# A gated two-layer block: inverse roots on GpSimd, scatters without pacing, and 8-bit rounding in the feed-forward

## The chip, the cores and the metric

The kernel runs on one core of a Trainium2 chip. The metric is the device time of one launch in microseconds (us). The kernel before takes 2155.1 us, the median of 3 runs (2150.84 to 2159.89).

Engines go by their short names: PE is TensorE (PEld its weight loads), DVE is VectorE, ACT is ScalarE, POOL is GpSimd, SP is SyncE. Each runs its own stream of instructions in program order and waits on semaphores that other engines raise.

## The reference

64 blocks of 128 tokens with 256 features, and as much context, go through two layers, each an attention over the context and a feed-forward:

```python
x = x + tanh(g_xattn[0]) * L0_xattn(layernorm(x), ctx, ctx)       # 16 heads of 16, softmax over 128 keys
x = x + tanh(g_ffn[0])   * L0_ffn(layernorm(x))                   # 64 experts, top 8, capacity 256, shared expert
x = x + tanh(g_xattn[1]) * L1_xattn(layernorm(x), ctx, ctx, mask) # the same with a mask
x = x + tanh(g_ffn[1])   * L1_ffn(layernorm(x))                   # 8-bit fake quantisation, 704 inner features

def _layernorm(x): return (x - mean(x)) / sqrt(var(x) + 1e-5)
def _act_fake_quant(x, clip_factor):
    scale = sigmoid(clip_factor) * max(abs(x)) / 127.0
    return clip(round(x / scale), -128.0, 127.0) * scale
xq = _act_fake_quant(x, clip_x)
h = _act_fake_quant(silu(xq @ wq(w_gate).T) * (xq @ wq(w_up).T), clip_down)
out = h @ wq(w_down).T
```

## The kernel before

The program has five stages, one after the other.

- **Start and layer 1's attention (to about 980 us).** 64 blocks pass through a software pipeline. In each *slot* every engine does a different piece of work for a different block: a stage `m` has its scores, the stages from `k` to `u` each hold an older one. A slot, read from one `mt` reduce of DVE (L793, the row maximum of the scores) to the next, holds on PE: scores (L346), V projection (L445), head sums (L476), shared expert's down projection (L536), transposes (L410), a second copy of the scores, transposed (L363), transposes of the head output (L486), of the maxima (L379) and of the normalised rows (L496), Q and K projections (L430), output projection (L463/L465), shared expert's up projections (L513), router logits (L525), probabilities by values (L393), counts of tokens by expert (L547/L548). ACT copies PSUM to SBUF between them (`xn` L637, `vx` L627, `pay` L651, `xt` L602, `at` L669, `x2t` L678), takes the exponential (L594) and the router's `en` (L688). DVE has maxima, residuals, statistics and the router's top 8.
- **Scatters.** For each block POOL issues 8 indirect DMAs (L1922), one for each of a token's experts, that write 128 rows of 1 KB each into the experts' buffers. Before each of the 8 stands a wait on a different semaphore of PE (the list `steps`), so that the 8 are spread over the slot. Before the first scatter POOL clears the buffers (L1905, 16 DMAs of 1032 KB, in pairs of which each waits for the last) and then two accumulators (L1909).
- **The inverse root of the variance.** `inverses` (L861 on) works on 2 columns, one for the block that enters and one for a block that leaves attention. It adds epsilon (`var`, L870) and then takes 11 small DVE instructions: a bit trick for a first value and three Newton steps, each waiting for the last; the last gives `rstd` (L890). `nmr` (L894) follows, and ACT's `xn` and `pay` wait for it. The planner of the DVE stream is the hand-written `body`: `norming(n)` puts n of these steps at a place, `routing(n)` n of the router's steps, `dispatching()` one of the three that turn counts into row numbers.
- **Experts (about 980 to 1270 us)**, with a scatter-add of results (L1407).
- **Layer 2's attention (about 1280 to 1930 us)** is the same pipeline without router, shared expert and scatters, and with a mask added on PE (L330). POOL has one small addition for each block (L1936).
- **Feed-forward, pass 0 (about 1935 to 2055 us)**, 16 chunks of 512 tokens: ACT scales by the quantiser's factor and adds 12582912.0, by which fp32 rounds; POOL clips and subtracts the constant again (two instructions over 128x2048, the second writes bf16); PE computes gate and up; DVE has three products and three maxima of the hidden values for each chunk.
- **Feed-forward, pass 1 (about 2057 to 2149 us)**, per chunk: ACT scales and rounds six slices of the hidden values (L1649); for four of them DVE adds the lower bound and subtracts the constant (`floored`, L1699, two instructions), then caps (L1708); for the other two POOL clips (L1674) and ACT subtracts (L1657); PE does 24 matmuls (L1736); DVE scales the result (L1716, four instructions), POOL adds the residual (L1680, four).

The wait that paces the scatters, and the order of DVE's stream around the root:

```python
steps = (("qk_done_0", ahead(b, 7)), ("o_done_0", ahead(b, 4)), ...
for n in range(TOPK):
    pool.wait_ge(sem(steps[n][0]), steps[n][1])
    G.indirect_dma_start(...)
...
variances(n, y); norming(5); routing(1); norming(2); routing(1); norming(2); routing(1); norming(1)
silu(w); norming(2); silu_up(w); norming(1)
```

## Time and profile before

| | us |
|---|---|
| median of 3 runs | 2155.1 |
| profiled execution, its own time | 2150.62 |
| its span in the profile | 2148.9 |
| mean granted TensorE clock | 0.954 of full |
| PE busy | 1825.1 (85%) |
| DVE busy | 1583.3 (74%) |
| ACT busy | 1117.6 (52%) |
| POOL busy | 900.0 (42%) |

"Span" is the time from the first to the last instruction that the profile has; the execution's own time is 1.7 us longer. Busy time is an average over stages with different limits, so the stages have to be read apart. In rows of the time line the bracket says how long the engine was idle before the instruction, and what it waited for; `remote` is a releaser that the profile does not name, `issue` an engine that waited for nothing that the profile shows.

### The profile page before, as it was taken

Reading aid. Unit: us, or ns where it says so; the run is one execution under the profiler, and the core shown is the slowest. Engines: PE = TensorE matmul, PEld = TensorE weight load, DVE = VectorE, ACT = ScalarE, POOL = GpSimd, SP = SyncE. Lnnn points to the kernel's source line nnn. Section 1 sums busy time; section 2 is a strip of 40 time slices with the busy share of each in tenths; the row PEclk is TensorE's granted clock in tenths of the full one; section 3 lists DMA queues with packets and bytes.
Section 4 is the critical chain, followed back from the end, with each engine's and each line's share of the span. In section 5 each row is a group of like instructions: output and inputs, shape, how many; then the busy total and the mean of one; then the engine's idle time right before and its main releaser. Section 6 shows DMA issues by size and latency. Waiting matters only on the chain.

```text
span 2148.9 us, 56605 instructions
## 1 busy us (share of the span) xinstructions
PE 1825.1 (85%) x20848; PEld 1451.8 (68%) x20848; DVE 1583.3 (74%) x6070; ACT 1117.6 (52%) x2299; POOL 900.0 (42%) x844
## 2 busy tenths in 40 slices
PE   5998888888889889746999978999999999968856
PEld 3777777777777777636888856676676667643334
DVE  5788888888888888772444447787887878778977
ACT  2555555555555555412222225666666666648877
POOL 1255555555555555574777750000000000005558
PEclk8999999999999999967999989999999999999988
DMA  9821111121111111045999951111111111102355
GB/s 234 217 80 56 53 51 48 48 68 53 41 36 43 43 42 38 22 138 127 225 210 219 208 102 40 46 39 45 40 41 43 39 46 39 31 24 108 127 204 188
DMA packets 184178, 187.98 MB, mean 87 GB/s; under 512 B 37042, under 2 KB 166613, under 8 KB 181856
## 3 DMA queue, kind: packets, MB, share of 16 engines
q1 hardware_dynamic: 136384, 142.69, 21.5%
q0 software_dynamic: 47520, 41.67, 10.5%
q8 instruction: 168, 2.75, 0.5%
q14 instruction: 106, 0.87, 0.1%
HBM read 103.72 MB, written 140.77 MB: 114 GB/s over the span
## 4 chain that ended last, share of the span: by engine, by line
PE 35%; DVE 30%; another core or an unknown queue 10%; issue 9%; DMA 7%; ACT 4%; POOL 4%; SPq 1%; POOLq 0%; ACTq 0%; DVEq 0%
DVE mt L793 8%; DMA accumulator<-ye,tid 6%; PE bank L513 5%; PE tiles L363 4%; PE bank L393 4%; PE tiles L346 3%; PE bank L476 3%; PE bank L465 2%; PE bank L445 2%; DVE hmax L1617 2%; POOL accumulator L1407 2%; PE bank L536 2%; DVE qm L805 2%; DVE newton L880 2%
## 5 line engine op out<-in xcount | busy, mean ns | idle before, releaser
L1922 POOL DMA_INDIRECT expert_rows<-pay,idx x512 | 503.7, 984 | 374.8 <-issue 107.8
L793 DVE TENSOR_REDUCE mt<-tiles 128x16 f32<-128x2048 f32 x128 | 293.5, 2293 | 49.6 <-PE tiles L346 37.1
L1936 POOL TENSOR_TENSOR res<-res,bias 128x256 f32<-128x256 f32 x64 | 46.3, 724 | 573.4 <-ACT xn L637 573.4
L594 ACT ACTIVATE pt<-tiles 128x2048 f32<-128x2048 f32 x128 | 241.6, 1887 | 44.3 <-PE tiles L363 44.1
L1407 POOL DMA_INDIRECT accumulator<-ye,tid x128 | 198.5, 1551 | 93.7 <-DMA accumulator<-ye,tid 34.8
L617 ACT ACTIVATE qkp<-bank,kb,keep 128x128 f32<-128x128 f32 x500 | 205.1, 475 | 0.0
L363 PE MATMUL tiles<-qm,qkp 32*128 32x128 f32 x4096 | 152.6, 286 | 40.1 <-DVE mt L793 36.9
L363 PEld LDWEIGHTS tiles<-qm,qkp 32*128 32x128 f32 x4096 | 127.8, 188 | 69.3 <-DVE mt L793 50.3
L430 PE MATMUL bank<-xt,w_q 128*128 128x128 f32 x1024 | 167.1, 287 | 3.2 <-issue 2.2
L393 PE MATMUL bank<-pt,vx 128*32 128x128 f32 x4096 | 160.2, 277 | 11.1 <-issue 9.1
L430 PE MATMUL bank<-cxax,w_k 128*128 128x128 f32 x1000 | 156.8, 279 | 0.6 <-issue 0.6
L669 ACT COPY at<-bank 128x256 f32<-128x256 f32 x128 | 47.7, 372 | 210.5 <-remote 183.7
L805 DVE SCALAR_TENSOR_TENSOR qm<-bank,keep,qkp 128x256 f32<-128x256 f32 x256 | 112.1, 479 | 59.0 <-remote 54.6
L430 PEld LDWEIGHTS bank<-xt,w_q 128*128 128x128 f32 x1024 | 138.6, 196 | 25.0 <-issue 23.1
L346 PE MATMUL tiles<-qkp 32*128 32x256 f32 x2048 | 150.1, 407 | 2.9 <-ACT qkp L617 2.9
L445 PE MATMUL bank<-w_v,cxax 128*128 128x256 f32 x500 | 137.5, 398 | 3.1 <-DMA res<-in_x 3.1
L1372 DVE TENSOR_SCALAR ye<-bank,wcol 128x256 f32<-128x256 f32 x128 | 56.0, 479 | 113.1 <-PE bank L1263 112.5
L393 PEld LDWEIGHTS bank<-pt,vx 128*32 128x32 f32 x4096 | 114.7, 110 | 34.8 <-issue 15.7
L430 PEld LDWEIGHTS bank<-cxax,w_k 128*128 128x128 f32 x1000 | 135.1, 195 | 1.8 <-issue 1.5
L465 PE MATMUL bank<-w_o,at 128*128 128x256 f32 x512 | 134.6, 386 | 0.5 <-ACT at L669 0.5
L660 ACT COPY ovs<-bank 128x512 f32<-128x512 f32 x128 | 75.1, 587 | 92.5 <-PE bank L393 92.5
L346 PEld LDWEIGHTS tiles<-qkp 32*128 32x128 f32 x2048 | 93.6, 187 | 27.7 <-issue 17.7
(263 smaller groups left out, 4175.0 us busy)
## 6 DMA issues: line engine op xcount, KB each, us to landing
expert_rows<-zt POOLq DMA_DIRECT2D x16, 1032.0 KB
xr<-expert_rows SPq DMA_DIRECT2D x64, 258.0 KB
cxax<-in_ctx SPq DMA_DIRECT2D x128, 128.0 KB
cxax<-accumulator SPq DMA_DIRECT2D x128, 128.0 KB, 2.2
hidden_away<-h_ring SPq DMA_DIRECT2D x8, 1536.0 KB, 5.0
res<-in_x SPq DMA_DIRECT2D x64, 128.0 KB
accumulator<-xa SPq DMA_DIRECT2D x64, 128.0 KB
accumulator<-zt SPq DMA_DIRECT2D x64, 128.0 KB
```

The lines of the kernel that those rows point to most:

```text
L346: last = nc.tensor.matmul(both, qt[r % 2][rows, j, :], kp[r][rows, :, j, :], start=(L == 0), stop=True, skip_group_check=(L == 1))
L363: last = nc.tensor.matmul(tiles[:, i, n * P:(n + 1) * P], kp[r][rows, e, j, :], qm[rows, e, j, :], start=(L == 0), stop=True, skip_group_c ...
L393: last = nc.tensor.matmul(bank[7][32 * h:32 * h + 32, g * P:(g + 1) * P], vx[r][:, GH * g + h, :], pt[p][:, i, n * P:(n + 1) * P], start=T ...
L430: last = nc.tensor.matmul(o_, w[:, c, j * P:(j + 1) * P], (cx[r] if n else xt[p])[:, c, :], start=(c == 0), stop=(c == KC - 1))
L445: last = nc.tensor.matmul(bk[:, 0:D], cx[r][:, c, :], w_v[:, c, :], start=(c == 0), stop=(c == KC - 1))
L465: last = nc.tensor.matmul(bank[6][:, 0:D], at[r % 2][:, c, :], w_o[:, c, :], start=(L == 1 and c == 0), stop=(c == KC - 1))
L594: nc.scalar.activation(pt[r % 2][:, :, :], tiles[:, :, :], ACT.Exp).then_inc(sem(sm("exp_done")), 1)
L617: last = nc.scalar.activation(kp[r][:, e, j, :], bank[5][:, (KC + j) * P:(KC + j + 1) * P], ACT.Identity, bias=kb[:, e, j:j + 1], scale=ke ...
L793: nc.vector.tensor_reduce(mt[:, :].rearrange("p (i n c) -> p i n c", i=RT, n=2 * KC)[:, :, :, 0], tiles[:, :, :].rearrange("p i (n k) -> p ...
L805: last = nc.vector.scalar_tensor_tensor(qm[:, e, :, :], bank[4 if L == 0 else 6][:, 0:P].unsqueeze(1).broadcast_to([P, KC, P]), keep[:, 1 ...
L1407: nc.gpsimd.indirect_dma_start(out=acc[p][:, :], out_offset=bass.IndirectOffsetOnAxis(ap=tid[r][:, h:h + 1], axis=0), in_=ye[r][:, h, :], ...
L1922: G.indirect_dma_start(out=xe[:, :], out_offset=bass.IndirectOffsetOnAxis(ap=idx[r][:, n:n + 1], axis=0), in_=pay[r][:, :], in_offset=None ...
```

## The change

Four parts.

1. **Inverse roots.** The 11 Newton instructions on DVE go, in both layers. DVE computes `var`; POOL takes `var` to the power -0.5 (one `tensor_tensor` with `ALU.pow` on 128x2, L1844) and DVE waits for it ahead of `nmr`. In the first layer POOL's stream has the power of the entering block ahead of the scatters of the block six slots older; in the second it stands ahead of L1936's addition.
2. **Scatters.** The waits on PE in front of them go; the only one left is for the block's row numbers. The clears of the experts' buffers are spread over the first slots between the powers, two pairs ahead.
3. **Order in layer 1.** PE's counts (now L549/L550) move behind the scores, into bank 5 and one slot later; V's projection (L447) moves behind the head sums (L478), into bank 4, and now waits for `silu_done` and `qm_done`; the transposes wait for `v_out` in their place. DVE takes the `mt` maximum ahead of the dispatch steps, and the router's steps stand earlier (8 of them in a row before the residual).
4. **Feed-forward.** ACT writes rounded values directly as 8-bit integers, which rounds and clips; the addition of 12582912.0, POOL's clips, and ACT's L1657 go. POOL turns pass 0's integers into bf16 with one copy instead of two instructions; in pass 1 DVE has three copies (of two slices each, 128x1024) in place of L1699's two and L1708's one. In pass 1 the stages also lie one chunk closer together.

```diff
             def transposes(f):
...
                 if L == 0:
-                    wait(pe, sm("silu_done"), b - 4)
-                    wait(pe, sm("qm_done"), b - 1)
+                    pe.wait_ge(sem(sm("v_out")), b + 1)
...
             def body(stage):
...
                 if L == 0:
+                    moe_counts(u)
+                    heads_to_tokens(o)
                     project_v(f)
-                    heads_to_tokens(o)
                     moe_down(v)
...
                     values(k)
-                    moe_counts(v)
@@ inverses
                 st.mark(V.tensor_scalar(var[:, :], mv[:, :, 1], EPS, None, ALU.add))
                 yield
-                st.need()
-                st.mark(V.tensor_scalar(root[:, :].bitcast(i32), var[:, :].bitcast(i32), 1, None, ALU.arith_shift_right))
...
+                dve.wait_ge(sem(sm("rstd_step")), NORM_STEPS * s1 + 2)
+                st.k += 1
                 st.mark(V.scalar_tensor_tensor(nmr[:, :], mv[:, :, 0], -1.0, rstd[:, :], ALU.mult, ALU.mult))
@@ DVE body, layer 1, then layer 2
-                    routing(3)
+                    routing(1)
...
-                    routing(5)
+                    routing(8)
...
                     variances(n, y)
-                    norming(5)
-                    routing(1)
...
                     norming(1)
+                    routing(1)
                     silu(w)
-                    norming(2)
                     silu_up(w)
                     norming(1)
...
                     variances(n, y)
-                    norming(11)
+                    norming(1)
                     shifted(m)
-                    norming(2)
+                    norming(1)
@@ POOL
+            def inverse_roots(eng, L, s):
+                if s >= NB + PAIR[L]:
+                    return
+                eng.wait_ge(sem(f"rstd_step_{L}"), NORM_STEPS * s + 1)
+                wait(eng, f"xn1_done_{L}", min(s, NB))
+                wait(eng, f"xn2_done_{L}", s - PAIR[L])
+                G.tensor_tensor(rstd[:, :], var[:, :], minus_half[:, :], ALU.pow).then_inc(sem(f"rstd_step_{L}"), 1)
...
                 for n in range(TOPK):
-                    pool.wait_ge(sem(steps[n][0]), steps[n][1])
                     G.indirect_dma_start(out=xe[:, :], ...
...
-            attention_slots(lambda stage: scatter(stage(6)))
+            for s in range(FIRST[0], NB + LAGS):
+                inverse_roots(pool, 0, s - FIRST[0])
+                zero_rows(s - FIRST[0] + ZEROED_AHEAD)
+                if s >= LAGS:
+                    scatter((s - LAGS, (s - LAGS) % 4))
@@ feed-forward
-                nc.scalar.activation(slot_of(k)[:, i, :], slot_of(k)[:, i, :], ACT.Copy, bias=RND, scale=s_guq[:, i:i + 1]
+                if i % 2 == 0:
+                    wait(act, "f_whole", IC // 2 * (k - 2) + i // 2 + 1)
+                nc.scalar.activation(h_i[k % 2][:, i, :], slot_of(k)[:, i, :], ACT.Copy, scale=s_guq[:, i:i + 1]
...
-                nc.gpsimd.tensor_scalar(h, h, RND + QMAX, RND - QMAX - 1.0, ALU.min, ALU.max).then_inc(sem("f_clipped"), 1)
...
+                V.tensor_copy(f_q[k % 2][:, 2 * p:2 * p + 2, :], h_i[k % 2][:, 2 * p:2 * p + 2, :]).then_inc(sem("f_whole"), 1)
```

POOL's stream in the middle of layer 1, before: one block's eight scatters.

```order
L1922 DMA expert_rows<-pay,idx 16384x258 [waits qk_done_0,slot_step_0]
L1922 DMA expert_rows<-pay,idx 16384x258 [waits o_done_0]
L1922 DMA expert_rows<-pay,idx 16384x258 [waits up_done_0]
L1922 DMA expert_rows<-pay,idx 16384x258 [waits pv_done_0]
L1922 DMA expert_rows<-pay,idx 16384x258 [waits s_done_0]
L1922 DMA expert_rows<-pay,idx 16384x258 [waits down_done_0]
L1922 DMA expert_rows<-pay,idx 16384x258 [waits v_done_0]
L1922 DMA expert_rows<-pay,idx 16384x258 [waits st_done_0]
```

POOL's stream there in the changed kernel, two blocks.

```order
L1844 TENSOR_TENSOR rstd<-var,minus_half 128x2 [waits xn2_done_0,xn1_done_0,rstd_step_0]
L1868 DMA expert_rows<-pay,idx 16384x258 [waits slot_step_0]
L1868 DMA expert_rows<-pay,idx 16384x258 x7
L1844 TENSOR_TENSOR rstd<-var,minus_half 128x2 [waits xn2_done_0,xn1_done_0,rstd_step_0]
L1868 DMA expert_rows<-pay,idx 16384x258 [waits slot_step_0]
L1868 DMA expert_rows<-pay,idx 16384x258 x7
```

Eight scatters now stand in a row behind each power, with no wait on PE between them.

PE's stream at the start of a slot of layer 1, before, from the values (L393) to the transposes.

```order
L393 MATMUL bank<-pt,vx 32x128 x15
L547 MATMUL bank<-sel,strict_tri 128x64 [waits en_out_0,sel_done_0]
L548 MATMUL bank<-sel,ones_e 128x64
L346 MATMUL tiles<-qkp 128x2x128 [waits qk_out_0,exp_done_0]
L346 MATMUL tiles<-qkp 128x2x128 x3
L346 MATMUL tiles<-qkp 128x2x128 [waits qk_out_0]
L346 MATMUL tiles<-qkp 128x2x128 x3
L445 MATMUL bank<-w_v,cxax 128x256 [waits qk_out_0,tile_in0]
L445 MATMUL bank<-w_v,cxax 128x256
L476 MATMUL bank<-ident,ovs 128x128 [waits ov_out_0]
L476 MATMUL bank<-ident,ovs 128x128 x3
L536 MATMUL bank<-w_sd,ht 128x256 [waits pos_done_0,silu_done_0]
```

The same stretch in the changed kernel.

```order
L397 MATMUL bank<-pt,vx 32x128 x15
L350 MATMUL tiles<-qkp 128x2x128 [waits qk_out_0,exp_done_0]
L350 MATMUL tiles<-qkp 128x2x128 x3
L350 MATMUL tiles<-qkp 128x2x128 [waits qk_out_0]
L350 MATMUL tiles<-qkp 128x2x128 x3
L549 MATMUL bank<-sel,strict_tri 128x64 [waits qk_out_0,sel_done_0]
L550 MATMUL bank<-sel,ones_e 128x64
L478 MATMUL bank<-ident,ovs 128x128 [waits ov_out_0]
L478 MATMUL bank<-ident,ovs 128x128 x3
L447 MATMUL bank<-w_v,cxax 128x256 [waits qm_done_0,silu_done_0,tile_in0]
L447 MATMUL bank<-w_v,cxax 128x256
L538 MATMUL bank<-w_sd,ht 128x256 [waits en_out_0,silu_done_0]
```

The counts no longer stand between the values and the scores, and V's projection is behind the head sums.

## Rows read from the trace of the kernel before

**Rows 1.** Windows: slots of layer 1 (56 together in one), of layer 2, two chunks.
```profile
core 0: us, PE busy (x) PEld busy (x) DVE busy (x) ACT busy (x) POOL busy (x), PEclk, DMA share, GB/s
85.07:96.64 11.57, 11.57 (x143) 10.19 (x144) 10.92 (x58) 7.31 (x17) 2.44 (x4) 1.00 0.75 197
96.64:115.01 18.37, 15.23 (x143) 12.80 (x144) 11.80 (x59) 6.97 (x16) 10.72 (x11) 0.81 0.37 127
502.23:515.96 13.73, 12.20 (x144) 10.41 (x143) 11.43 (x58) 7.19 (x16) 7.80 (x9) 1.00 0.17 46
115.01:890.37 775.36, 689.49 (x7953) 587.24 (x7954) 638.05 (x3191) 405.09 (x898) 435.93 (x449) 1.00 0.17 48
1499.59:1509.45 9.86, 9.20 (x147) 6.89 (x146) 7.88 (x27) 6.30 (x13) 0.73 (x1) 1.00 0.15 42
2124.55:2134.88 10.33, 7.05 (x48) 5.33 (x48) 8.29 (x16) 9.47 (x14) 9.79 (x10) 0.83 0.31 103
```

**Rows 2.** Time line, POOL, first train of scatters; start, duration, idle before.
```profile
96.52 1.08 POOL L1922 DMA_INDIRECT expert_rows<-pay,idx  x1 [0.30 <-issue]
...
104.33 0.97 POOL L1922 DMA_INDIRECT expert_rows<-pay,idx  x1 [0.31 <-issue]
...
505.18 0.97 POOL L1922 DMA_INDIRECT expert_rows<-pay,idx  x1 [1.24 <-PE bank L536]
```

**Rows 3.** Time line, ACT, around the same scatters.
```profile
89.09 0.37 ACT L669 COPY at<-bank 128x256 f32<-128x256 f32 x1 [1.10 <-PE bank L486]
...
99.19 0.37 ACT L602 COPY xt<-bank 128x256 f32<-128x256 f32 x1 [0.65 <-issue]
106.61 0.37 ACT L669 COPY at<-bank 128x256 f32<-128x256 f32 x1 [7.05 <-remote]
...
508.15 0.37 ACT L669 COPY at<-bank 128x256 f32<-128x256 f32 x1 [3.30 <-remote]
```

**Rows 4.** Time line, PE, inside the first train.
```profile
100.19 0.44 PE L486 MATMUL bank<-ident,on 128*128 128x128 f32 x2
...
103.60 0.39 PE L430 MATMUL bank<-xt,w_q 128*128 128x128 f32 x2 [0.94 <-issue]
```

**Rows 5.** Source view of L669, all of ACT's waits before it.
```profile
  remote: 183.7, 54
```

**Rows 6.** Time line, POOL and ACT, the last slots of layer 1.
```profile
918.14 0.97 POOL L1922 DMA_INDIRECT expert_rows<-pay,idx  x1 [1.24 <-PE bank L393]
...
925.80 0.97 POOL L1922 DMA_INDIRECT expert_rows<-pay,idx  x1 [0.30 <-issue]
...
928.22 0.22 ACT L688 ACTIVATE en<-bank 128x64 f32<-128x64 f32 x1 [7.17 <-remote]
```

**Rows 7.** Time line, DVE, where layer 1 ends a variance.
```profile
511.62 0.17 DVE L870 TENSOR_SCALAR var<-mv 128x2 f32<-128x2 f32 x1
```

**Rows 8.** Time line, DVE and PE, one slot of layer 2.
```profile
1506.32 0.17 DVE L870 TENSOR_SCALAR var<-mv 128x2 f32<-128x2 f32 x1
...
1508.39 0.88 DVE L805 SCALAR_TENSOR_TENSOR qm<-bank,keep,qkp 128x256 f32<-128x256 f32 x2
...
1507.29 1.15 PE L346 MATMUL tiles<-qkp 32*128 32x256 f32 x16
...
1511.80 0.44 PE L330 MATMUL tiles<-mask_bias,identb 32*32 32x512 bf16 x16 [0.51 <-DVE mt L793]
```

**Rows 9.** The page's costliest groups, an elementwise operation of POOL.
```profile
L1936 POOL TENSOR_TENSOR res<-res,bias 128x256 f32<-128x256 f32 x64 | 46.3, 724 | 573.4 <-ACT xn L637 573.4
```

**Rows 10.** Source views of pass 1: DVE L1708, POOL L1680, ACT L1657.
```profile
L1708 DVE TENSOR_SCALAR xq_f<-xq_f x8: 695/1102/1104, 2061.0 to 2132.8; 128x2048 bf16<-128x2048 bf16 x8
L1708 DVE TENSOR_SCALAR f_sgp<-f_sgp x8: 1409/1410/1436, 2066.4 to 2138.8; 128x2048 bf16<-128x2048 bf16 x8
...
L1680 POOL TENSOR_TENSOR xq_b<-xq_b,res x24: 716/726/1201, 2067.3 to 2144.8; 128x256 f32<-128x256 f32 x24
...
L1657 ACT ACTIVATE f_sgp<-big x6: 1057/1057/1057, 2077.6 to 2139.7; 128x1024 bf16<-128x1024 f32 x6
```

179 lines of the change are left out of this document (64 added, 115 removed).

## The prediction

> **What bounds the kernel now.** I read the windows first, because the page's shares mix five stages. In layer 1 the slot is the unit. Before any scatter runs, a slot takes 11.57 us and PE is busy for all of it [rows 1]. The 56 slots that begin at 115.01 take 775.36 us together, 13.85 each, with PE busy 689.54 / 56 = 12.31 [rows 1]: there PE is still the busiest, but 1.5 us of each slot belong to nobody. Between them lies one slot of 18.37 us. Three questions follow, and the other views answer them.
>
> *What is special about the slot of 18.37 us?* POOL had been held by the clears, so all the PE events that its scatters wait for had long happened. From 96.52 to 104.33 it issues seven in a row, 1.3 us apart [rows 2]. This is the only full unpaced train beside work at full rate, and so the nearest thing in this trace to what the change makes of every slot. Its TensorE clock fell to 0.81 of full, the 1.2 GHz level in part of it; in the clean slot it was 1.00.
>
> *What waited?* The head output's transpose on PE (L486) began at 100.19 and took 0.44. ACT's copy of it (L669) began at 106.61 after 7.05 us of idleness that the profile puts down to `remote`; in the clean slot the same wait was 1.10 [rows 3, 4]. PE, too, had gaps with no releaser, such as 0.94 us before 103.60. My reading is that a semaphore that PE raises while scatters are being written becomes visible late, most often when the queue of scatters has drained. The drain fits: two scatters issued from 505.18, at 1.43 to 1.5 us each, end at about 508.1, and ACT's copy starts at 508.15; seven issued from 918.14 end at about 928.2, and `en` starts at 928.22 after 7.17 us [rows 2, 3, 6]. The copy at 99.19 did get through, so in a train's first three microseconds something still passes.
>
> *How much of this is paid today?* The remote waits before L669 alone sum to 183.7 us in 54 cases [rows 5], 3.4 each, of which about 2 lie over the clean wait of 1.10. That is about the 13.85 − 11.57 = 2.3 us by which a paced slot is longer than a clean one.
>
> Layer 2's slot is 9.86 us. There the row maximum starts only when DVE has come through its stream, and PE then waits 0.51 us for it ahead of the masks [rows 1, 8]. In pass 1 two chunks take 10.33 us; ACT is busy 9.47 and POOL 9.79 of them [rows 1].
>
> **The change, part by part.**
>
> *Scatters without pacing.* POOL gets the power of the entering block, then eight scatters. The power needs `var`, and `var` ends at 511.79 [rows 7], 3.6 us after the held copy at 508.15, since the output projection and the second statistics lie between them. So the train starts some 3.6 to 4.7 us after the hold ends, and the next one cannot start earlier, because its power waits for the same chain. Eight scatters at 1.43 us are 11.4 us of drain. If the copy waits for the drain each time, a slot is 11.4 + 4.3 = 15.7 us. The upper bound is the observed 18.4 for seven scatters, plus 1.3 for the eighth, less what the clearer DVE stream gives back: 19. PE's own stalls in the train (15.23 busy of 18.37 at the lower clock) lie in between. I take 17.0, between the two. Of the 64 trains one is the first, 57 stand in full slots and six in slots that empty the pipeline. For the 57 that is 57 × (17.0 − 13.85) = +180 us. The first was unpaced already (−1), and the last six, with little left to cover a train, give about +20, taken as 3.3 each like the others. Layer 1: **+200**.
>
> *The root in layer 1.* Eleven DVE instructions of about 0.2 us leave a slot in which DVE is busy 11.43 of 13.73 [rows 1]; the slot is not bound by them, so I give nothing. Their cover is the hold itself: without it, PE's 11.57 is the next bound, and DVE's 11.43 − 2.2 = 9.2 lies below that. The power is one POOL instruction of 128x2. The nearest POOL row is an addition of 128x256 at 724 ns [rows 9]; below stands 0.15, the length of such an instruction on DVE, as the `var` row shows [rows 8]. I take 0.5; both ends are shorter than the 2.1 us removed. What is queued behind it on POOL is the train, and ACT's `xn` and `pay` wait for `nmr`.
>
> *Clears and order.* The clears land at their own pace in either kernel and their cover is the first slots: 0. Counts behind scores: the scores of a slot no longer wait for `en`, worth at most 0.2 us a slot, and I count it inside the rounding of 17.0. V's projection now waits for DVE's `silu_up` and `qm` and has PE's scores ahead of it as cover; without that cover DVE's last 0.4 us instruction would be paid.
>
> *The root in layer 2.* `var` starts at 1506.32 and `qm` at 1508.39 [rows 8]; with one short wait in place of eleven instructions `nmr` and `mt` could come 2.1 us earlier, but the scores end at 1507.29 + 1.15 = 1508.44, which lets `mt` move from 1509.45 by 1.0 at most, and PE idles only 0.51. After that PE is the bound. Gain 0.5 × 62 slots = 31, and 5 for the slots that fill and empty: **−36**. Bounds: 0 if the power takes 2 us or more, −60 if all of 1.0 counts.
>
> *Pass 1.* ACT loses L1657, 1.06 us of each chunk [rows 10]; what is left of its 9.47 us in two chunks is 3.7 each, against a chunk of 5.17 now. POOL loses the clip and keeps four additions at 0.72 = 2.9. DVE has 8.29 / 2 = 4.1 a chunk, and its L1708, twice the size of the others, becomes one of three equal copies, so 3.5 to 4.1; more if it is held up, for L1708 takes 1.410 us in half of its instances and 0.695 at its fastest [rows 10]. Between 3.7 and 5.1 I take 4.5, since PE and DVE still hand each chunk to one another: 16 × 0.67 = 11, and one for the shorter tail: **−12**, range −23 to −2.
>
> The Trainium skill has a rule against this part: in "SBUF — State Buffer", section "Who interferes with whom", DVE in a two-port mode, which copies and casts use, and a GpSimd instruction exclude each other. By it the chunk would be an estimated 3 × 0.68 + 4 × 0.72 = 4.9 us and the gain 4 us; the 1.410 of L1708 beside POOL's work, against 0.695 at its fastest, agrees with it [rows 10].
>
> *Pass 0.* POOL's two instructions become one, ACT's stay, DVE's six products and maxima still fill the chunk: **−1**, for the first chunk.
>
> **Sum.** 2150.6 + 200 − 36 − 12 − 1 = 2302 for the profiled execution, whose time is 4.5 us below the median; so **2306 us** in the terms of the median. A measurement of this kernel tells 0.5% (11 us) from no change.
>
> **The rivals.**
>
> *A: pacing buys nothing.* The hold costs per scatter, not per train: 2.3 us a slot are paid today with eight spread scatters. A train of eight held at one place might also fall where little waits, behind the values, so that the slot stays at 13.85 − 0.2. Then only the gains remain, and the drained slots: 2155 − 57 × 0.2 − 49 = **2095**. For it: the first copies inside the train passed. Against it: 18.37 in the one slot that shows it. It decides from the point where a train costs less than 2.3 us of waits. This is the case on the other side of no change.
>
> *B: the hold goes.* If what delays PE's semaphores is the pacing's own waits on PE, or the slot of 18.37 was long through the end of the clears (0.37 DMA share, against 0.17 later [rows 1]) and the lower clock, then the slot falls back to about 11.6 to 12: 57 × 2.0 = −114, with −49 for the rest and −7 for the first slot: **1985**. Against it: seven scatters at 918.14, with no clear anywhere near, gave the same 7.17 us [rows 6].
>
> The Trainium skill, "SBUF — State Buffer", section "Who interferes with whom", says that PE and ACT never wait on anyone and that DMA traffic does not contend with a compute engine; by that rule trains would be free, and B would follow. The trace does not agree so far: ACT waited 7.05 us [rows 3].
>
> *C: the power is slow.* From about 2 us (layer 2) or 4 us (layer 1) a power on POOL delays `nmr`, hence `xn`, `pay` and the next slot; at 5 us layer 2 alone loses 3 × 62 = 186 us: over 2400.
>
> *D: half.* Trains cost 1 us a slot more, and the gains pay for that: 2155. That the change doesn't do what it says can hardly be: the order shows the trains without waits.
>
> **Chances.** The forecast (slots of 15.7 to 19, 2220 to 2400) 0.55; A 0.25; B 0.10; C 0.05; D 0.05, of which 0.04 within 0.5%. Faster than by 0.5%: A, B and 0.01 of D, 0.36. Same 0.04. Slower 0.60. The forecast's own range is 2220 to 2400. The range with 2 in 10 left out drops B and C and reaches A: **2070 to 2400**.
>
> **What would show it.** In the changed profile: layer 1's slots by their `mt` reduces (17 expected; 13.7 for A, 12 for B); eight POOL scatters 1.27 apart behind each power; ACT's `at` copy with 6 us or more of `remote` ahead of it, in nearly every slot, and starting 11.4 us after the train's first scatter; the granted clock in those slots, which I expect under 1.00. In layer 2 slots of 9.3 with PE's idle time ahead of the masks gone. In pass 1, chunks of 4.5, and DVE's copies at 0.7 or at 1.1 and more. If slots of layer 1 are under 14.5, my reading of the train is wrong, whatever the total. If POOL's power takes more than 1 us, so is that bound.

## The result, and the profile after

The changed kernel took 2531.7 us (median of 4 runs, 2526.3 to 2533.2), against 2154.5 beside it: 1.174 of the time before, 95% interval 1.171 to 1.178. It was slower, as forecast, but by 377 us where 151 were forecast, and outside the range (2070 to 2400).

The windows below cut both profiles at the first and last row maximum (`mt`) of each layer. Columns: the stretch, its length, busy time and instructions of each engine, granted TensorE clock, DMA share. First the kernel before:

```profile
core 0: us, PE busy (x) PEld busy (x) DVE busy (x) ACT busy (x) POOL busy (x), PEclk, DMA share, GB/s
31.90:890.40 858.50, 762.53 (x8766) 648.73 (x8767) 698.67 (x3447) 447.67 (x991) 458.26 (x474) 0.98 0.24 64
890.40:1284.80 394.40, 310.85 (x1939) 273.36 (x1938) 183.34 (x696) 96.62 (x243) 256.87 (x183) 0.89 0.74 168
1284.80:1904.20 619.40, 572.20 (x9005) 428.00 (x9005) 489.39 (x1552) 387.81 (x799) 44.89 (x62) 0.99 0.14 42
1904.20:2148.90 244.70, 169.56 (x1093) 94.90 (x1093) 198.97 (x304) 179.73 (x254) 133.79 (x110) 0.88 0.36 138
```

Then the changed kernel, and one slot of its first layer:

```profile
29.80:1319.00 1289.20, 913.69 (x8772) 767.12 (x8772) 600.86 (x2752) 452.13 (x991) 509.30 (x538) 0.80 0.16 43
1319.00:1723.00 404.00, 316.48 (x1931) 278.10 (x1931) 173.16 (x632) 97.07 (x243) 258.09 (x187) 0.86 0.73 164
1723.00:2301.70 578.70, 564.23 (x9005) 425.48 (x9005) 386.27 (x859) 388.47 (x799) 88.19 (x124) 1.00 0.15 44
2301.70:2530.80 229.10, 157.39 (x1093) 88.07 (x1093) 195.78 (x258) 163.90 (x237) 76.22 (x83) 0.94 0.38 147
463.09:484.77 21.68, 15.10 (x143) 12.86 (x142) 9.86 (x46) 7.37 (x16) 8.12 (x9) 0.83 0.10 28
```

The stretches are the first layer from its first `mt` to its last, the end of that layer with the experts, the second layer, and the end of its pipeline with the feed-forward. The first layer went from 858.5 to 1289.2 us: **+430.7**. The experts' stretch went from 394.4 to 404.0 (+9.6), the second layer from 619.4 to 578.7 (−40.7), the last stretch from 244.7 to 229.1 (−15.6). With −2.1 at the start that is the 381.9 us between the two spans. The last stretch splits by the first starts of ACT's scaling in pass 0 and in pass 1 (1934.7 and 2057.6 before, 2325.4 and 2447.6 after): the end of layer 2's pipeline went from 30.5 to 23.7 us (−6.8), pass 0 from 122.9 to 122.2 (−0.7), pass 1 from 91.3 to 83.2 (−8.1). In the first layer PE's busy time also rose, from 762.5 to 913.7 us for the same instructions, with the granted clock at 0.80 of full in place of 0.98: part of the stretch ran at the 1.2 GHz level. The first six slots have no scatters yet and take 66.4 us together; the 57 behind them take 21.45 on average ((1319.0 − 96.2) / 57), and the one shown 21.7.

Where the time goes is to be seen in that slot. POOL has the power and then the train:

```profile
476.75 0.72 POOL L1844 TENSOR_TENSOR rstd<-var,minus_half 128x2 f32<-128x2 f32 x1 [11.54 <-DVE var L872]
477.66 1.03 POOL L1868 DMA_INDIRECT expert_rows<-pay,idx  x1 [0.19 <-issue]
...
486.68 0.97 POOL L1868 DMA_INDIRECT expert_rows<-pay,idx  x1 [0.30 <-issue]
```

DVE ended the variance just ahead of it; the next maximum came eight microseconds later:

```profile
476.50 0.17 DVE L872 TENSOR_SCALAR var<-mv 128x2 f32<-128x2 f32 x1
...
484.77 2.29 DVE L795 TENSOR_REDUCE mt<-tiles 128x16 f32<-128x2048 f32 x1 [5.90 <-remote]
```

PE had long done what that maximum and ACT's copies wait for:

```profile
467.20 0.66 PE L413 MATMUL bank<-ident,xn 128*128 128x128 f32 x2 [3.81 <-ACT vx L629]
467.79 2.09 PE L367 MATMUL tiles<-qm,qkp 32*128 32x128 f32 x32
...
477.29 1.08 PE L397 MATMUL bank<-pt,vx 128*32 128x128 f32 x32
478.30 1.15 PE L350 MATMUL tiles<-qkp 32*128 32x256 f32 x16
...
482.30 1.03 PE L447 MATMUL bank<-w_v,cxax 128*128 128x256 f32 x4
```

```profile
466.69 0.37 ACT L629 COPY vx<-bank 128x256 f32<-128x256 f32 x1 [6.83 <-remote]
...
481.17 0.58 ACT L662 COPY ovs<-bank 128x512 f32<-128x512 f32 x1 [3.28 <-remote]
...
489.07 0.37 ACT L629 COPY vx<-bank 128x256 f32<-128x256 f32 x1 [6.81 <-remote]
```

PE's first rows of the slot show it idle for 3.81 us and then slow: 32 matmuls of L367 take 2.09 us there, at a granted clock of 0.50, the 1.2 GHz level, for 1.17 us where it is granted in full (so in a_paced at 522.28). Values (L397) end at 477.29 + 1.08 = 478.37, and ACT's copy of them starts at 481.17. Scores (L350) end at 479.45, and the maximum starts at 484.77. V's projection (L447) ends at 483.33, and its copy starts at 489.07, which is 11.4 us after the train's first scatter at 477.66: eight times 1.43, as the rows of before had it [rows 2, 3]. So each event came 2.8 to 5.7 us late, and V's copy, the last of them, came at the end of the train. Then nothing is held until the next train. From the released copy at 466.69 to the end of the variance at 476.67 are 10.0 us, with the power 1.0 more until the train, and then 11.4 until the next release: 22.4 from one V copy to the next (466.69 to 489.07), a slot's whole chain.

This holds for nearly every slot. In 52 of the 57 trains V's copy starts 11.4 to 11.6 us after the first scatter. The way from V's copy to the end of the variance takes 9.06 us in the median, so that the chain is 11.4 + 9.1 + 1.0 = 21.5, the average slot. This way is longer than on a chip where the clock stays up: the changed kernel's run after_3, below, has 7.3 to 7.6 us for the same work in most slots, 7.48 in the median. The stretch in this profile, then in after_3's:

```profile
466.69:476.67 9.98, 9.47 (x75) 8.83 (x76) 5.58 (x36) 5.78 (x12) 0.00 (x0) 0.66 0.18 54
```

```profile
508.43:515.76 7.33, 7.33 (x82) 6.79 (x80) 7.09 (x43) 5.62 (x12) 5.63 (x6) 1.00 0.28 75
```

PE is busy for almost all of it in both, at 0.66 and at 1.00 of the clock. An estimate from the two medians: 57 × 1.6 = 90 us of the +430.7 come through the lower clock that follows PE's idle time in the hold, and not through the waits themselves.

The source view of V's copy (L629) has the sum of the waits:

```profile
L629 ACT COPY vx<-bank x125: 350/373/399, 18.1 to 2296.3; 128x256 f32<-128x256 f32 x125
...
  remote: 345.9, 52
```

345.9 us are `remote` in 52 waits, 6.7 each; [rows 5] had 183.7 in 54, at the copy of the head output.

Two lines for the smaller terms. The power on POOL has a price now, for 128x2:

```profile
L1844 POOL TENSOR_TENSOR rstd<-var,minus_half x138: 688/706/737, 13.0 to 2321.2; 128x2 f32<-128x2 f32 x138
```

DVE's copies in pass 1 take 0.68 us at their fastest (the first four start before any of POOL's additions, and take 0.69) and 1.21 in the median; L1708 had such a spread too [rows 10]. Two chunks take 9.28 us (from the cast at 2466.38 to that at 2475.66), 4.64 each:

```profile
L1645 DVE CAST f_sgp<-wui x24: 682/1210/1232, 2452.7 to 2522.0; 128x1024 bf16<-128x1024 int8 x24
```

### The profile page after: what moved, and what is told of

Same layout as the page of the kernel before. It is cut to its first block, busy times and chain, and to the rows that moved or that the text cites. A ratio compares the mean times of both kernels' runs of the same rounds, so it can differ in the third digit from the quotient of the medians.

```text
span 2530.8 us, 55163 instructions
## 1 busy us (share of the span) xinstructions
PE 1963.6 (78%) x20848; PEld 1566.9 (62%) x20848; DVE 1365.4 (54%) x4551; ACT 1107.5 (44%) x2283; POOL 940.7 (37%) x952
## 4 chain that ended last, share of the span: by engine, by line
PE 47%; another core or an unknown queue 23%; DVE 11%; DMA 7%; issue 6%; ACT 4%; POOL 2%; SPq 0%; POOLq 0%; ACTq 0%; DVEq 0%
PE bank L432 10%; PE tiles L367 7%; PE bank L515 5%; DMA accumulator<-ye,tid 4%; DMA expert_rows<-zt 3%; PE bank L397 3%; PE tiles L350 3%; PE bank L467 2%; PE bank L447 2%; PE tiles L1222 2%; DVE hmax L1583 2%; PE tiles L334 2%; PE bank L478 2%; DVE h_ring L1576 1%
## 5 line engine op out<-in xcount | busy, mean ns | idle before, releaser
L1844 POOL TENSOR_TENSOR rstd<-var,minus_half 128x2 f32<-128x2 f32 x138 | 97.8, 708 | 1040.1 <-DVE var L872 1039.8
L413 PE MATMUL bank<-ident,xn 128*128 128x128 f32 x256 | 64.1, 341 | 231.0 <-ACT vx L629 223.4
L367 PE MATMUL tiles<-qm,qkp 32*128 32x128 f32 x4096 | 199.8, 347 | 11.0 <-DVE mt L795 11.0
L629 ACT COPY vx<-bank 128x256 f32<-128x256 f32 x125 | 48.0, 384 | 361.0 <-remote 345.9
L413 PEld LDWEIGHTS bank<-ident,xn 128*128 128x128 f32 x256 | 34.1, 167 | 266.6 <-issue 263.4
L367 PEld LDWEIGHTS tiles<-qm,qkp 32*128 32x128 f32 x4096 | 169.8, 244 | 45.6 <-issue 31.5
L478 PE MATMUL bank<-ident,ovs 128*128 128x128 f32 x512 | 85.1, 289 | 126.9 <-ACT ovs L662 106.9
L432 PEld LDWEIGHTS bank<-xt,w_q 128*128 128x128 f32 x1024 | 160.0, 223 | 30.6 <-issue 28.8
L616 ACT ACTIVATE qkp<-bank,qb 128x128 f32<-128x128 f32 x256 | 95.1, 373 | 141.0 <-PE bank L432 140.8
L350 PE MATMUL tiles<-qkp 32*128 32x256 f32 x2048 | 150.1, 405 | 2.9 <-ACT qkp L619 2.8
L447 PE MATMUL bank<-w_v,cxax 128*128 128x256 f32 x500 | 151.7, 433 | 0.0
L478 PEld LDWEIGHTS bank<-ident,ovs 128*128 128x128 f32 x512 | 54.4, 142 | 142.9 <-ACT ovs L662 114.8
```

The costliest lines, as they stand in the source:

```text
L350: last = nc.tensor.matmul(both, qt[r % 2][rows, j, :], kp[r][rows, :, j, :], start=(L == 0), stop=True, skip_group_check=(L == 1))
L367: last = nc.tensor.matmul(tiles[:, i, n * P:(n + 1) * P], kp[r][rows, e, j, :], qm[rows, e, j, :], start=(L == 0), stop=True, skip_group_c ...
L432: last = nc.tensor.matmul(o_, w[:, c, j * P:(j + 1) * P], (cx[r] if n else xt[p])[:, c, :], start=(c == 0), stop=(c == KC - 1))
L447: last = nc.tensor.matmul(bank[4][:, 0:D], cx[r][:, c, :], w_v[:, c, :], start=(c == 0), stop=(c == KC - 1))
L478: last = nc.tensor.transpose(bank[7][:, g * P:(g + 1) * P], ov[r % 2][:, g, :], ident[:, :])
```

## The experiments

All ratios are against the kernel before, timed beside it on the same chip. The five sets of runs met five different chips, and that became the main finding; the kernel before took 2160 and 2162 us on the chips of the first and third set, and 2021, 2015 and 2013 us on those of the second, fourth and fifth. "A chip with holds" is short for one of the first sort; by its 2154.5 us before, the chip of the result was one too. No chip was met twice, so it is not shown that the sort belongs to the chip, and not to something else that held while a set ran.

### First set: what makes the slot long

**Scatters paced again** (label a_paced):

```diff
+                steps = (("qk_done_0", ahead(b, 7)), ("o_done_0", ahead(b, 4)), ...
                 for n in range(TOPK):
+                    pool.wait_ge(sem(steps[n][0]), steps[n][1])
                     G.indirect_dma_start(...)
```

> The changed kernel with the eight waits on PE put back in front of the scatters, nothing else. Theory T (a train of scatters holds PE's semaphores until it has drained, and the next train starts only after the power, about 11 us after the release): without trains the first layer's slot goes back to 13 to 14.5 us from 21.4, and the kernel to 2080 to 2150 us. Rival R (the power on POOL, or the moved V projection and counts, are what lengthens the slot): the slot stays over 18 us and the time over 2350.

Measured: 2255.4 us, 1.043 of before (1.039 to 1.047), and 276 us below the changed kernel. The missing waits are most of the loss, but putting them back does not lead back to before. POOL's rows show why:

```profile
513.01 0.72 POOL L1844 TENSOR_TENSOR rstd<-var,minus_half 128x2 f32<-128x2 f32 x1 [5.48 <-DVE var L872]
513.92 1.04 POOL L1871 DMA_INDIRECT expert_rows<-pay,idx  x1 [0.19 <-issue]
...
516.53 0.97 POOL L1871 DMA_INDIRECT expert_rows<-pay,idx  x1 [0.30 <-issue]
518.26 0.97 POOL L1871 DMA_INDIRECT expert_rows<-pay,idx  x1 [0.75 <-remote]
```

The power stands in POOL's stream and comes only with the variance; the next scatters' waits have been met by then, so they leave in a little train of three, 1.3 us apart. The pacing works only if nothing else holds POOL back. Slots of 13.6 us and of 17.6 to 22 alternate in this way up to the last train, long after the clears, 16.8 on average where 13 to 14.5 were expected. So 1.043 is neither theory's number: theory T is right on the direction, and its 2080 to 2150 left this out.

**The kernel before without pacing** (b_unpaced):

```diff
                 for n in range(TOPK):
-                    pool.wait_ge(sem(steps[n][0]), steps[n][1])
                     G.indirect_dma_start(...)
```

> The kernel before with the eight waits on PE taken out, nothing else: the Newton steps, PE's order and the clears stay. Theory T: trains hold PE's semaphores here too; the train starts when the row numbers are ready, so fewer microseconds lie between release and next train than behind the power: slots of 16 to 20 us, 2280 to 2520 in all. Rival R: slots stay under 15 and the time under 2220.

Measured: 2526.9 us, 1.170 (1.166 to 1.175), with slots of 20.4 us on average; both lie a little above theory T's upper bounds (20 and 2520). This edit alone, with Newton, old order and old feed-forward, loses as much as the whole change. The train is the same, and ACT's `en` waits for its end:

```profile
495.94 0.97 POOL L1921 DMA_INDIRECT expert_rows<-pay,idx  x1 [10.43 <-DVE idx L1035]
...
504.88 0.97 POOL L1921 DMA_INDIRECT expert_rows<-pay,idx  x1 [0.30 <-issue]
```

```profile
507.48 0.22 ACT L688 ACTIVATE en<-bank 128x64 f32<-128x64 f32 x1 [6.69 <-remote]
```

495.94 + 8 × 1.43 = 507.4; `en` starts at 507.48 after 6.69 us. Rival R is out. In this kernel the train meets PE in the middle of the values (L393), and PE's own stream slows down too, though it waits for nothing that the profile shows:

```profile
501.37 0.64 PE L393 MATMUL bank<-pt,vx 128*32 128x128 f32 x14
502.36 0.27 PE L393 MATMUL bank<-pt,vx 128*32 128x128 f32 x1 [0.35 <-issue]
...
505.92 0.31 PE L393 MATMUL bank<-pt,vx 128*32 128x128 f32 x2 [1.10 <-issue]
507.35 1.08 PE L393 MATMUL bank<-pt,vx 128*32 128x128 f32 x11 [1.11 <-issue]
```

Some of these matmuls start 0.71 us apart, others 1.43, which is also the time for one scatter, and the group takes 7.1 us in place of 1.08. Over the kernel there are 299 such gaps before L393, 207.2 us in all, against 25 and 9.1 us in the kernel before. So a train can hold PE's matmuls as well as its semaphores. Which of the two comes first, and by what mechanism, no run shows.

**The first layer of before, the rest changed** (c_layer1_old):

```diff
-    NORM_STEPS = 13
+    NORM_STEPS = (13, 3)
...
+                if L == 0:
...
+                else:
+                    dve.wait_ge(sem(sm("rstd_step")), NORM_STEPS[L] * s1 + 2)
+                    st.k += 1
```

> The kernel before with only the second layer's power and the 8-bit feed-forward; the first layer is untouched. Both theories: the gains of these two parts alone. From the changed kernel's trace the second layer's slot is 9.27 against 9.86 us (62 slots, -37) and a chunk of pass 1 is 4.64 against 5.17 (-9 with the tail): 2105 to 2112 us. Over 2130 would say that part of these gains is only made up of something that the first layer gives.

Measured: 2099.3 us, 0.972 (0.966 to 0.978): 61 us less than beside it (49 to 73 by the interval), where the terms of the expectation sum to 46; they left out the 6.8 us at the end of layer 2's pipeline. The two parts keep their gain by themselves.

**The changed kernel with PE's old order** (d_order), and DVE's dispatch steps ahead of the maximum again:

```diff
-                    moe_counts(u)
-                    heads_to_tokens(o)
                     project_v(f)
+                    heads_to_tokens(o)
...
                     values(k)
+                    moe_counts(v)
```

> The changed kernel with PE's order of before in the first layer: counts between values and scores, V's projection ahead of the head sums in bank 5, and the waits that belong to it; DVE's dispatch steps ahead of the maximum. Scatters stay unpaced behind the power. Theory T, with the place of the hold: V's copy passes earlier in the train, and the hold falls on a later step (the copy of the head output), about 4 us ahead of the variance, so the slot shrinks from 21.4 to 15.5 to 18 us, in all 2190 to 2340. Rival (any place costs the same, since every event of PE in the train is held to its end): slot 20 to 22, 2450 to 2570.

Measured: 2551.8 us, 1.180 (1.176 to 1.185). My theory on the place of the hold fell, and the rival stood: with V's projection back ahead, its copy waits just as long (347.2 us in 52 waits, for 345.9 in 52), and the slot is 21.7 us on average. The maximum waits somewhat less, and the dispatch steps, now ahead of it, take 170.9 us of such waits themselves. The group of the maximum, in the changed kernel and in this one:

```profile
L795 DVE TENSOR_REDUCE mt<-tiles 128x16 f32<-128x2048 f32 x128 | 293.5, 2293 | 438.3 <-remote 360.2
```

```profile
L797 DVE TENSOR_REDUCE mt<-tiles 128x16 f32<-128x2048 f32 x128 | 293.5, 2293 | 367.4 <-remote 294.8
```

### Second set: how much it depends on the number and the distance of the scatters

**Work of POOL's own between scatters** (g_gap):

```diff
                 for n in range(TOPK):
+                    G.memset(spare[:, :], 0.0).then_inc(sem("gap"), 1)
+                    pool.wait_ge(sem("gap"), 8 * b + n + 1)
                     G.indirect_dma_start(...)
```

> The changed kernel with a small piece of POOL's own work (a fill of a spare 128x256 tile, waited for) in front of each of the eight scatters; no wait on another engine. It adds work and takes none away. Theory T1 (backlog: scatters are issued 1.27 us apart and written in about 1.43, so the queue never empties in a train, and PE's semaphores get through only when it is empty): with 1.6 to 1.9 us between scatters the queue empties after each, holds fall under 1.5 us, the slot falls from 21.4 to 14.5 to 16.5 us (POOL: 8 x 1.8 + 0.9), and the kernel to 2130 to 2270 us although POOL has more to do. Theory T2 (PE's semaphores are held from a train's first scatter to its last, whatever lies between): the train is 13 to 15 us long in place of 10.2, the slot grows to 24 to 26 us and the time to 2650 to 2800.

Measured: 2343.3 us, 1.160 (1.159 to 1.162), but the kernel before took 2021 us beside it, not 2155, so the bounds of the expectation do not apply. Slots are 17.4 us, and POOL's work fills them. A gap with its wait came to 0.8 us, more than I had allowed: scatters are 2.08 us apart in place of 1.6 to 1.9.

**Half of the scatters** (h_half) and **none** (n_none), `range(TOPK // 2)` and `range(0)` in the same loop:

> The changed kernel with four of the eight scatters of a block (the other four of each token's experts get no rows). T1 and T2 alike: the slot is 10 us from the release to the variance, 1 for the power, and 1.43 for each scatter less what passes before the first hold: 21.4 - 4 x 1.43 = 15.7 us, the time 2531 - 57 x 5.7 = 2205, plus or minus 40. If a train costs a fixed amount however long it is, the time stays over 2400; if only a queue of more than four matters, it falls under 2100.

> The changed kernel with no scatters of rows at all (experts get no rows): what all scatters cost together, and the first layer's floor with the power on POOL. If nothing but the scatters lengthens the slot, it is 11.2 to 11.8 us, as in the slots of either kernel before the first scatter, and the time 1945 to 1990 us. If the power or the moved projection costs by itself, the slot is over 12.5 and the time over 2030.

Measured: 1925.7 and 1927.3 us, one run each; they leave out rows that the experts need, and serve for the time alone. Four scatters in a train cost nothing at all here, where 2205 was expected, and with none the time is 18 us under its expectation (1945 to 1990), with the slots of 11.4 us that it named. That fitted neither theory until the traces showed that on this chip no wait of ACT before `vx`, `at` or `ovs` is `remote`.

**Newton and paced scatters, all else changed** (e_newton_paced): the changed kernel with `inverses` and POOL's stream of c_layer1_old, which are those of before in the first layer, and with the new order of PE and of DVE's maximum.

> The changed kernel's PE order in the first layer (counts behind the scores, V's projection behind the head sums), second layer and feed-forward, but with the Newton steps on DVE, the clears ahead and the paced scatters in the first layer. It differs from the run with the whole first layer of before (2099 us) by the PE order alone, and from the paced run with the power (2255 us) by where the root is taken. If what made that one slow is the power that stands in POOL's queue between scatters and so bunches them, the time here is 2080 to 2130; if it is the PE order, it is 2200 to 2270.

Measured: 1948.7 us, 0.964 (0.963 to 0.966). The numbers in the expectation were meant for a chip with holds, so this run does not decide between its two causes; e_2, below, does.

### Third set: the same kernels on another chip

> The changed kernel once more, unaltered. The runs since show two sorts of chip: on one (kernel before 2155 to 2160 us) PE's semaphores are held in a train of scatters, on the other (kernel before 2021 us) none is held, with or without gaps. Theory C (the hold belongs to the chip, and is the whole loss): on a chip where the kernel before takes about 2021 us the first layer's slot is 11.2 to 11.8 us and this kernel 1925 to 1950, faster than before; on one where it takes about 2155, 2520 to 2540 again. Rival: trains hold PE on both, only less there: over 2050 on the first sort.

> The kernel before, unaltered, for a profile on the same chip. Theory C: where it takes about 2021 us, ACT's waits before the copy of the head output that the profile puts down to remote are gone (under 10 us in all, against 183.7), and the slot is 11.6 to 12 us in place of 13.85; where it takes about 2155 they are there again, 170 to 195 us.

> The kernel with Newton steps on DVE, paced scatters and the changed kernel's PE order in the first layer, second layer and feed-forward as changed: 0.964 of before on the chip without holds. On a chip without holds: again 0.955 to 0.97, and 5 to 25 us above the changed kernel. On a chip with holds: its pacing was laid out for the old order, so holds are a little longer than before's; 0.965 to 1.01 of before, and more than 300 us below the changed kernel.

> The changed kernel with a waited-for fill ahead of each scatter, which makes scatters 2.1 us apart. On a chip without holds POOL binds again: slots of 18 us, 2335 to 2350 in all. On a chip with holds it tells backlog from presence: if PE's semaphores are held only while scatters queue up, it is the same 2335 to 2400 there, less than the changed kernel; if held through any train, over 2600.

Measured, on a chip with holds (before 2162.5 us): the changed kernel 2534.2, 1.171 (1.166 to 1.176); the kernel before 2163.3 in one more run; Newton and paced 2099.4, 0.969 (0.966 to 0.973), which is what the old PE order gave (0.972), so the order is worth nothing that can be told here, and what a_paced (2255.4) loses beyond it comes with the power in POOL's stream; the gaps 2337.4, one run. The source view of the copy of the head output, kernel before:

```profile
L669 ACT COPY at<-bank x128: 372/372/373, 51.4 to 1935.8; 128x256 f32<-128x256 f32 x128
...
  remote: 189.1, 54
```

189.1 us again. The run with gaps is the telling one. It has more for POOL to do than the changed kernel and is 197 us faster, and it takes as long as on the chip without holds (2337 and 2343). Its rows:

```profile
510.78 0.97 POOL L1871 DMA_INDIRECT expert_rows<-pay,idx  x1 [0.78 <-POOL spare L1869]
511.75 0.33 POOL L1869 MEMSET spare<- 128x256 f32 x1
512.86 0.97 POOL L1871 DMA_INDIRECT expert_rows<-pay,idx  x1 [0.78 <-POOL spare L1869]
```

```profile
512.30 0.59 ACT L663 COPY ovs<-bank 128x512 f32<-128x512 f32 x1 [0.71 <-PE bank L398]
```

```profile
L796 DVE TENSOR_REDUCE mt<-tiles 128x16 f32<-128x2048 f32 x128 | 293.5, 2293 | 72.9 <-PE tiles L351 72.9
```

Scatters start 2.08 us apart. Values (L398 there, 510.98 + 1.08) end at 512.06 in the middle of this, and ACT's copy starts at 512.30, not 2.8 us later; nothing in the maximum's idle time is `remote`. The slot is 17.4 us, which is POOL's own time, 8 × 2.08 + 0.8. So scatters beside PE's events do no harm as such; scatters 1.28 us apart do. That this is because their queue never empties, each taking about 1.43 us, fits these numbers but is an inference: the gap also adds a wait of POOL on itself, and no run separates the two.

### Fourth and fifth set: smaller gaps, and the changed kernel on a chip without holds

**Pairs** (k_pairs, k_pairs_2) and **two trains of four** (k_one): the fill is replaced by a power on two columns of a spare tile, for which nobody waits.

```diff
                     G.indirect_dma_start(...)
+                    if n in (1, 3, 5):
+                        G.tensor_tensor(spare[:, b % 8, (1, 3, 5).index(n), :], ones2[:, :], minus_half[:, :], ALU.pow)
```

> The changed kernel with a small power of POOL's own (on a spare tile, waited for by nobody, 0.7 us) behind the second, fourth and sixth scatter: pairs 1.27 us apart with 0.9 us between pairs. T1 (only a queue that never empties holds PE's semaphores): the queue empties after each pair, holds are under 3 us, POOL's work of 0.9 + 8 x 1.28 + 3 x 0.9 = 13.9 us sets the slot: 13.9 to 15 us, 2531 - 57 x 7 = 2130 +- 40 on a chip with holds, and about 2070 +- 30 on one without. T2 (presence of scatters): over 2450 on a chip with holds.

> The same with one such gap, behind the fourth scatter: two trains of four. T1: PE's events of the first half are held to 0.5 us behind the fourth scatter, and those of the second half again, each hold up to 5 us: slot 15 to 19 us, 2200 to 2400 on a chip with holds; POOL's 12.0 us sets it on one without: 1950 to 1970. If half trains did nothing, the place is the chain's alone and it stays over 2480.

> The changed kernel with four of the eight scatters of a block, once more (on the chip without holds it took 1926 us, as much as with none). On a chip with holds T1 and T2: 10 us from release to variance, 1 for the power, and a train of four, 5.7 less 0.7: slot 15.7, 2205 +- 40. If the hold grows out of the backlog that 1.27 against 1.43 leaves, four scatters have 0.6 us of it where eight have 1.3, and the slot is under 13, the time under 2050.

> The changed kernel with no scatters of rows (on the chip without holds 1927 us, slots of 11.4). Theory C: the chips differ in the holds alone, so this takes 1920 to 1940 us on a chip with holds too. If it is over 2000 there, the chip is slower in something else as well.

> The changed kernel, unaltered, a third time. Theory C: if the kernel before takes about 2015 to 2021 us beside it (a chip without holds), this takes 1925 to 1950 us, with slots of 11.4 to 11.7 and PE as their bound: the change then makes the kernel faster by 4%. If before takes about 2155 to 2163 us (a chip with holds), it is 2525 to 2540 as twice before.

> The changed kernel with its scatters in pairs, 0.9 us of POOL's own work between pairs; 2048 us on the chip without holds. On a chip with holds, T1 (a queue that empties holds nothing for long): within 60 us of that, 2048 to 2110, below the kernel before. T2 (presence): over 2450. On a chip without holds: 2045 to 2052 again.

Measured, all on chips without holds (before 2015.5 and 2012.7 us): pairs 2048.1 and 2045.5, 1.016 and 1.015, 22 us under the middle of the first expectation and inside the second, with slots of 12.97 us; two trains of four 1957.9, 0.972 (0.970 to 0.973), as expected for such a chip; half of the scatters 1924.2 and none 1924.6, one run each; and the changed kernel, unaltered, **1941.4 us, 0.964 (0.961 to 0.967)**. No run with pairs met a chip with holds, so what they do there stays open; so does what two trains of four, four scatters and none do there.

The changed kernel on that chip, the first layer and one slot of it:

```profile
core 0: us, PE busy (x) PEld busy (x) DVE busy (x) ACT busy (x) POOL busy (x), PEclk, DMA share, GB/s
29.00:746.60 717.60, 706.80 (x8765) 624.65 (x8766) 593.13 (x2751) 447.39 (x991) 504.49 (x533) 0.99 0.29 78
118.90:130.31 11.41, 11.41 (x145) 10.13 (x144) 9.65 (x47) 7.24 (x17) 8.86 (x10) 1.00 0.38 123
```

```profile
505.62 1.03 POOL L1868 DMA_INDIRECT expert_rows<-pay,idx  x1 [0.30 <-issue]
506.96 0.97 POOL L1868 DMA_INDIRECT expert_rows<-pay,idx  x1 [0.30 <-issue]
```

```profile
505.88 0.58 ACT L662 COPY ovs<-bank 128x512 f32<-128x512 f32 x1 [0.54 <-PE bank L397]
...
508.43 0.37 ACT L629 COPY vx<-bank 128x256 f32<-128x256 f32 x1 [1.46 <-PE bank L447]
```

```profile
L629 ACT COPY vx<-bank x125: 350/372/400, 18.1 to 1705.1; 128x256 f32<-128x256 f32 x125
...
  PE bank L447: 88.5, 61
```

The train is the same, 1.3 us apart. But values that end at about 505.8 are copied at 505.88 after 0.54 us, V's copy starts at 508.43, in the middle of the train, and none of its waits is `remote`. The slot is 11.41 us with PE busy for all of it at the full clock.

## Why the prediction was right or wrong

*That trains hold PE's semaphores, and that this is the loss:* right for the chip of the result. That the trains are the loss is shown by one edit (b_unpaced, 1.170) and by its undoing in part (a_paced, 1.043). That they act on PE's semaphores is read from the waits; in b_unpaced they also slow PE's own matmuls, of which the prediction had seen a trace (0.94 us) and made no term. The clock in these slots was under 1.00, as expected, and that had no term of its own either: about 90 us, by the estimate above.

*The length of the hold, 11.4 us for eight scatters:* right for the last held event; V's copy starts 11.4 to 11.6 us after the first scatter in 52 of 57 trains. But no single event is held that long, and earlier ones pass inside the train: the values' copy 3.5 us and the maximum 7.1 us after its start.

*The step that failed* is "the train starts some 3.6 to 4.7 us after the hold ends". I took the copy of the head output, at which the hold ended in the slots of before, for the place where it ends in the train too. But the train now begins behind the variance, so that its hold covers the start of the slot: the values' copy, the maximum and V's copy. From V's copy to the next train lie the transposes, the scores' second copy, the head output, Q and K, the output projection and the variance: 9.1 us in the median (10.0 in the slot shown), and 1.0 for the power. The train starts 10.1 us after the release and not 3.6 to 4.7, and the sum should have been 11.4 + 10.1 = 21.5, which is the average slot of 21.45. The term was 57 × (17.0 − 13.85) = +180; with the measured slot it is 57 × (21.45 − 13.85) = +433. The +20 for the end was too much: the experts' stretch, in which the last trains fall, has +9.6. The upper bound of 19 came from a train that began at the maximum, further on in the slot, and so was no bound. d_order shows that PE's order alone does not mend this.

*The root in the second layer, −36:* −40.7, and −6.8 more at the end of its pipeline, inside the bounds of 0 and −60. The power took 0.71 us, inside its two ends, though above the 0.5 taken; the lower end was given as 0.15 from the `var` row, which reads 0.17 [rows 8]. The slot is 9.28 for 9.86.

*Feed-forward, −13:* −8.8, of which pass 0 has −0.7 (−1 forecast) and pass 1 −8.1 (−12 forecast). The last stretch as a whole has −15.6, but that nearness to −13 is chance, since 6.8 of it belong to layer 2. The chunk of 4.64 lies between the 4.5 of the sum and the estimate of 4.9, nearer the first; DVE is busy for 9.06 of the 9.28 us of two chunks, so its copies set the chunk, and they are the ones that were held up. The rule of the Trainium skill in "SBUF — State Buffer", section "Who interferes with whom", is that a copy or cast of DVE in a two-port mode and a GpSimd instruction exclude each other. This trace agrees: 0.69 us for the first four casts, without POOL's work, and 1.21 to 1.23 for two of three beside it.

*Rival A (pacing buys nothing, 2095):* wrong where the result was taken, on a chip with holds. On chips without holds pacing does buy nothing, as the rival's name says (e_newton_paced 0.964, changed kernel 0.964), but with slots of 11.4 and not of 13.65.

*Rival B (the hold goes, 1985):* it is what happens on the chips without holds, where 1941.4 was measured, with slots of 11.41 for the 11.6 to 12 of that case. Its cause was named wrongly: on a chip with holds, neither taking out the pacing's own waits (b_unpaced) nor the distance from the clears makes the hold go; it goes with the chip. The Trainium skill, "SBUF — State Buffer", section "Who interferes with whom", says that PE and ACT never wait on anyone. It says so of the memory's ports, and the prediction took it for the whole chip: these chips' traces agree (no `remote` wait), and the others' have waits for PE's semaphores, 345.9 us before V's copy alone, of which it does not speak.

*Rival C (a slow power):* no; 0.71 us.

The forecast spoke of one time. The profile of before could not tell that the same kernel is 2013 to 2021 us on other chips; the waits with no named releaser, 183.7 us before L669, and PE's gaps were the only signs.

## What to carry to other kernels

Where a semaphore's releaser ended long before its waiter starts and the profile says `remote`, ask what transfers were in flight, and take the place in the loop at which a burst begins as seriously as its length: the loss is the hold plus the chain from its end to the next burst. Indirect DMAs in a row should be spaced over the loop by waits that cost the issuing engine nothing: on a chip with holds this was worth 366 us (2160 us before, 2527 in b_unpaced), and on chips without, the paced e_newton_paced was no slower than the unpaced changed kernel (0.964 both). Gaps of the issuing engine's own work took the holds away too, but with 2337 us cost more than they saved against before. A wait put behind another dependency on the issuing engine undoes the spacing. And a kernel should be timed on more than one chip before such a trade is settled: here the sign of the change depends on it, while 8-bit rounding and the second layer's power, with the first layer left alone (0.972) or with its new order and Newton (0.969 and 0.964), win on each chip they ran on, the first on one chip with holds, the second on one of each sort.

## What the runs showed of the hardware that was not expected

- Two sorts of chip, two with holds and three without in the five sets, none met twice. On one, PE's semaphores were visible up to 6 us late while indirect DMAs followed each other 1.28 us apart; on the other never. The kernel before takes 2155 to 2163 us on the one and 2013 to 2021 on the other; the changed one 2532 to 2534 and 1941. The kernel with waited gaps takes 2337 and 2343, and the changed kernel's second layer and last stretch 578.7 and 229.1 us on the one, 578.6 and 230.1 on the other, so the chips differ in nothing else that these show. What makes the difference was not found; the packets of GpSimd's DMA queue, clears and the experts' scatter-add included, take the same time (8.9% of 2530.8 us and 11.7% of 1940.7, 225 and 227 us).
- On a chip that had the hold, it was gone with 2.08 us between scatters (g_2). That it is one of queueing is the reading that fits.
- A train slows PE's matmuls too: in b_unpaced 32 of them took 7.1 us for 1.08, in steps of 0.71 and 1.43 us.
- A power of 128x2 takes 0.71 us on GpSimd, as long as an addition of 128x256 [rows 9].
